# Local stage: the first pair of exponentials between ScalarE's two head-out copies; q and k written and read on SP ahead of both groups of P

## The reference

```
for l in range(DEPTH):                       # DEPTH = 2
    h = shift_token(x)
    q, k, v = split(h @ wqkv)                # 8 heads of 64
    q, k = rotary_xpos(l2norm(q) * qs, l2norm(k) * ksc)
    o = softmax(mask(8 * q @ k.T)) @ v       # windows of 128, each sees itself and the one before
    x = x + o @ wo
    h = layernorm(shift_token(x)) * lg + lb
    a, g = split(h @ w1 + b1)
    x = x + (a * gelu(g)) @ w2 + b2
```

## Time and profile before

| | |
|---|---|
| median of 3 runs | 4911.67 us (4908.47 to 4913.42) |
| the profiled execution | 4915.73 us, span 4913.9 us |
| PE busy | 4346.3 us, 88% of the span |
| DVE, ACT, POOL busy | 67%, 59%, 47% |
| DMA | 728.62 MB, mean 148 GB/s |

### The profile page before, as it was taken

The page is one execution under the profiler, slowest core; times in us unless marked ns, Lnnn a source line. Parts: engine busy times, 40 slices in busy tenths (PEclk is TensorE's granted clock), DMA queues, the critical chain, the costliest instruction groups (busy, mean ns, idle before and its releaser), DMA issues. The chain is left out here.

```text
span 4913.9 us, 281580 instructions
## 1 busy us (share of the span) xinstructions
PE 4346.3 (88%) x114072; PEld 3665.2 (75%) x114072; DVE 3295.8 (67%) x10277; ACT 2920.9 (59%) x8550; POOL 2290.3 (47%) x3196
## 2 busy tenths in 40 slices
PE   7888888678888888665999999999999999999998
PEld 6888888668888888653777777777777777777776
DVE  4666666578888888474666666666666666666664
ACT  5777777534444444253666666666666666666665
POOL 1222222257777777302444445444445555555553
PEclk8999999879999999787999999999999999999999
DMA  3334343467777777595666666666676667676665
GB/s 88 88 94 97 90 94 95 103 147 163 164 167 163 164 166 163 143 296 160 153 156 156 154 154 152 151 152 155 162 176 159 160 163 164 161 162 161 158 158 121
DMA packets 1454099, 728.62 MB, mean 148 GB/s; under 512 B 676624, under 2 KB 1398288, under 8 KB 1452816
## 3 DMA queue, kind: packets, MB, share of 16 engines
q1 hardware_dynamic: 1402448, 652.89, 57.6%
q10 hardware_dynamic: 51392, 73.02, 5.1%
HBM read 410.48 MB, written 315.15 MB: 148 GB/s over the span
## 5 line engine op out<-in xcount | busy, mean ns | idle before, releaser
L2354 ACT ACTIVATE l_prob<-l_prob,l_nb,l_rq 128x160 f32<-128x160 f32 x1024 | 518.4, 509 | 14.3 <-DVE l_nb L2189 14.3
L2015 POOL TENSOR_TENSOR l_k<-l_kn,l_tab 128x512 f32<-128x512 f32 x128 | 162.1, 1267 | 613.2 <-DVE l_kn L2163 613.2
L2031 POOL TENSOR_TENSOR l_prob<-l_prob,l_rinv 128x320 f32<-128x320 f32 x512 | 362.8, 719 | 76.3 <-DVE l_rinv L2171 76.1
L2559 PE MATMUL lD<-l_hid,w 128*128 128x128 f32 x3072 | 363.9, 275 | 0.0
L2559 PEld LDWEIGHTS lD<-l_hid,w 128*128 128x128 f32 x3072 | 353.3, 192 | 0.0
L2551 PEld LDWEIGHTS lA<-l_hn,w 128*128 128x128 f32 x2048 | 243.1, 195 | 110.3 <-POOL l_hn L2049 61.1
L2198 DVE STREAM_TRANSPOSE l_pb<-l_prob 128x320 f32<-128x320 f32 x512 | 250.6, 498 | 104.1 <-POOL l_prob L2031 104.1
L2025 POOL TENSOR_TENSOR l_qr<-l_q 128x512 f32<-128x512 f32 x128 | 162.4, 1269 | 329.0 <-DVE l_q L2127 329.0
L1097 POOL TENSOR_TENSOR sc_aqx<-sc_late,sc_headmask 128x256 f32<-128x256 f32 x256 | 172.1, 672 | 278.3 <-PE sc_Y L1190 275.0
L1173 PE MATMUL sc_AB<-sc_aq,sc_bkx 32*32 32x32 f32 x16384 | 258.6, 198 | 39.9 <-POOL sc_bkx L1097 29.7
L497 POOL TENSOR_TENSOR rk<-rk,bkraw 128x256 f32<-128x256 f32 x64 | 54.6, 872 | 477.8 <-DVE bkraw L383 477.8
(11 more groups left out here) (273 smaller groups left out, 13217.1 us busy)
## 6 DMA issues: line engine op xcount, KB each, us to landing
l_pT<-scratch_pz SPq DMA_DIRECT2D x1024, 128.0 KB, 3.7
scratch_pz<-l_pb SPq DMA_DIRECT2D x256, 320.0 KB, 3.0
scratch_qkz<-l_qk SPq DMA_DIRECT2D x128, 512.0 KB, 3.2
l_qkT<-scratch_qkz SPq DMA_DIRECT2D x512, 128.0 KB, 3.8
scratch_cm<-cm SPq DMA_DIRECT2D x64, 512.0 KB, 4.1
sc_early<-scratch_cm ACTq DMA_DIRECT2D x59, 512.0 KB
scratch_tok<-vt SPq DMA_DIRECT2D x512, 48.0 KB, 1.8
scratch_part<-sc_att SPq DMA_DIRECT2D x64, 384.0 KB
```

Of the source, the lines that this page charges most:

```text
L2015: tt(k1[s][:], kn[s][:], wide(2, slice(0, DH)), ALU.mult)
L2031: tt(prob[s][:, pair], prob[s][:, pair], rinv[s][:, pair].unsqueeze(2).broadcast_to([P, 2, SPAN]), ALU.mult).then_inc(Q["pn"][s].sem, 1)
L2354: last_ = nc.scalar.activation(prob[s][:, h], prob[s][:, h], ACT.Exp, scale=rq8[s][:, h:h + 1], bias=nb[s][:, h:h + 1], accum_out=sums[s][ ...
L2559: last_ = mm(bank[s][3][:, c * P:(c + 1) * P], w2[:, m, c * P:(c + 1) * P], hid[s][:, m], start=(c == 0 and m == 0), stop=(c == CC - 1 and ...
```

## The change

On SP the q and k write comes before both writes of P, and the q and k read before both reads of P. On ScalarE `exponent` 0 stands between `head_out` 0 and `head_out` 1.

```diff
@@ sync: half @@
-                    write_p(s, u, 0)
                     if within(un):
                         write_qk(o, un)
+                    write_p(s, u, 0)
                     write_p(s, u, 1)
-                    read_p(s, u, 0)
                     if within(un):
                         read_qk(o, un, wn)
+                    read_p(s, u, 0)
                     read_p(s, u, 1)
@@ scalar: half @@
                         head_out(o, um, 0)
+                    exponent(s, u, 0)
+                    if mlp:
                         head_out(o, um, 1)
-                    exponent(s, u, 0)
                     exponent(s, u, 1)
```

## The result

The changed kernel takes 4853.51 us, the median of 4 runs (4852.8 to 4857.42), beside 4910.07 for the kernel before in the same session (4905.67 to 4913.42). The ratio is 0.9886, with a 95% interval of 0.987 to 0.9902: faster, by 57 us. The forecast was 4856.

A forecast was written before the change was run, and what follows sets the result against it. PE, busy 88%, is bound by how early each local-stage half's projection can start, with P1 late. Period 20.18 to 19.68 over 127 halves saves 63.5 us, giving 4848; plus 8 for late landings, 4856; range 4840 to 4895.

The forecast's parts named there:

- rival 1: Local stage: PE's wait for P becomes a wait of 0.3 to 0.6 us for ACT's copy; 4840 to 4880, chance 0.70.
- `l_nb` sits under POOL's lock: VectorE's `l_nb` ends with POOL's rotation of k, 2.68 us into the half, which sets the floor of exponent 0.
- The part behind the projection: From the projection's start to the half's end, alike in both layers: 15.42 and 15.58 us, taken as unchanged.
- the term for late landings: Noise in when DMA reads land, P0 having 0.8 us to spare: half of today's 17.4 us, 8 us added.
- The sum of 19.68 x 127: New period of a half, 4.18 + (15.42 + 15.58) / 2 = 19.68 us against 20.18, over 127 halves: 63.5 us.
- Signs that the prediction named: `l_pT` wait under 15 us, ACT copy wait about 0.5 a half, projection at 4.2, period 19.7; wrong if values 0 await P0.
- When P lands: SP's DMA queue at 218 GB/s: P1 lands 1.5 us earlier, P0 with 0.8 us to spare before values 0.
- the bytes hold it, not the issues: P1's landing is set by 2.42 MB queued from the q/k write, 11.1 us at 218 GB/s, not by SP's issuing.
- Rival 2: Reads only partly in time: P0 some tenths late every half, mean 0.25 us, half the gain left; 4880 to 4901, chance 0.13.
- The swap alone gains nothing: ACT part, exponent 0 moved between the two `head_out` copies: no gain alone, free only while P1 is late.
- it holds back part of what SP gives: Without the ACT part the copy could start as soon as values 3 end, at 2.8 to 3.2 us.
- Rival 3: Slower: q/k write's early issue frees nothing, values 0 wait 0.7 us for P0 every half; 4937, chance 0.05.

The follow-up runs named there:

- e1_sp_only: Kernel before with only SP's new order of writes and reads, ScalarE's order as before: 4847.41 us, ratio 0.9867.
- e5_nb_one_input: Changed kernel with `l_nb` made by two one-column tensor_scalar instructions instead of one two-column tensor_tensor: 4855.22 us, ratio 0.9881.
- e7_rotate_order: Changed kernel with POOL's three products of rotate_k reordered, the two short ones first and the long one last: 4879.4 us, ratio 0.993.
- e15_xa_last: e3_early_write_only with the load of the residual x issued on SP behind both writes of P: 4866.75 us, ratio 0.9906.
- e3_early_write_only: Changed kernel with SP's reads back in the old order (P0, q/k, P1), q/k write still ahead of P0: 4880.16 us, ratio 0.9933.
- e4_early_read_only: Changed kernel with SP's writes back in the old order (P0, q/k, P1), reads still q/k, P0, P1: 5020.39 us, ratio 1.022.
- e8_k_turned_first: Changed kernel without the swap; `turn_k` ahead of `attended`, q/k write ahead of SP's window load, q/k read between P's writes: 4833.15 us, ratio 0.9835.
- e2_act_only: Kernel before with only ScalarE's new order (the swap), SP's order as before: 4914.28 us, ratio 1.0003.
- e10_both: e8_k_turned_first (no swap) with the `l_nb` of e5_nb_one_input: 4807.81 us, ratio 0.979.

## Why the prediction was right, and where its sizes were off

**The wait that takes over (rival 1)** is shown. P1 comes in time, exponent 0 starts when `l_nb` ends, and the copy behind it releases PE. I had 2.72 for exponent 0, 3.74 to 4.11 for the copy and 4.18 for the projection. The half above shows 2.72, 3.74 to 4.09 and 4.15, and the mean over all halves is 4.15 (4.69 before). e1_sp_only shows that it is the swap that sets 4.15 in layer 0, and e5_nb_one_input and e7_rotate_order that `l_nb` sets it in turn: with `l_nb` at 2.59, 2.66 and 2.81 the projection is at 4.09, 4.15 and 4.30 (means of all halves). In layer 1 the copy ends last by 0.04 us only. The prediction had PE's own work end at 3.54 + 0.37 = 3.91 there and the maxima of pair 1 in time; they are not, and without the swap the projection stands at 4.10. So what rival 1 says holds in full for one layer of the two.

**That `l_nb` sits under POOL's lock** was argued from two rows. The ends of all 381 long `l_nb` show it, and e5_nb_one_input supports it: with one column of one tile plus a column as scalar, `l_nb` finishes while POOL still runs. The prediction cited the Trainium skill, SBUF — State Buffer, section Who interferes with whom; by its rule that a VectorE instruction with at most one SBUF input, outside the 2-port modes, does not contend (if a column taken as a scalar is no such input) the two new instructions should keep their length under POOL's work, and they do: 0.34 us for both under `l_k`, against 0.44 for the one instruction of the change. How much earlier `l_nb` could be was not part of the forecast. With this remedy it is 0.09 us.

**The part behind the projection** was taken as 15.42 and 15.58, and it is in the middle: medians of the two kinds of halves are the same numbers. Its means are 15.58 and 15.71, because values 0 now and then wait for P0. That is about 0.14 us a half, 18 us in all, where the term for late landings had 8. The sum of 19.68 x 127 plus 8 us corresponds to a period of 19.74. Measured is 19.78.

**That the total came out within 3 us is in part luck.** A fall of the period from 20.18 to 19.78 over 127 halves is 51 us, and the local stage gave 56. The rest comes from halves at its ends, which the prediction did not look at: the first takes 22.28 us instead of 24.98. They make up for what the late P0 cost beyond its term of 8 us. What lies ahead of the local stage took 2 us less in this execution.

**Signs that the prediction named.** Exponent 0, the projection and the period are as it said. It allowed PE under 15 us of waits for `l_pT` in 2300 us; there are 16.5 and 13.5. It named a wait of values 0 for P0 as a sign that it is wrong, and there are 22 of them, up to 2.1 us. It had about 0.5 us a half for the wait on ACT's copy; PE's matmuls wait 10.5 us in all, 0.09 a half, and its weight load 46.1, 0.4 a half.

**When P lands** is the step that was mis-sized. I let bytes queue at 218 GB/s, so that 0.52 MB fewer in front of the reads were worth 2.4 us, and P1's landing moved 1.5 us towards the projection. It moved 0.6: P1 lands about 17.7 behind the projection's start (median; 18.3 before), and P0 at 15.1 to 15.2 instead of 14.6, which leaves it 0.3 of slack and not 0.8. What the runs show in its place is that P1 follows the first read at a distance that changes little with the bytes. Reads start at 7.8 before, 7.5 in the change, 8.07 in e15_xa_last (layer 1), 8.73 in e3_early_write_only (layer 1) and 9.27 in e4_early_read_only; P1 lands 10.5, 10.2, 9.9, 9.6 and 9.7 later. In e8_k_turned_first and the three kernels built on it the reads start at 5.8 to 6.0 and P1 lands 10.9 later. Getting the q/k write out of the way saved 0.3 us of that distance and 0.3 us of the start.

Two readings of the prediction failed with this. The rate was no constant: over the reads of the changed kernel the DMA engines are nearly as full as before (share 0.97 against 1.03) and move 191 GB/s, not the 218 of the earlier trace rows:

```profile
3235.00:3245.00 10.00, 9.71 (x125) 9.03 (x125) 6.63 (x23) 6.10 (x15) 3.20 (x4) 1.00 0.97 191
```

And "the bytes hold it, not the issues" is too strong. SP issues the last read of P1 5.4 to 5.5 us behind the first read in the change (5.9 before, 7.1 to 7.4 in e8_k_turned_first), and P1 lands 4.5 to 4.7 us behind that (4.5 before, 3.5 to 3.7 in e8_k_turned_first). In the change 1.91 MB move between first read and landing in layer 0 and 2.18 in layer 1, and the distance is the same in both (medians). No run changes the pace of the issues alone, so how much of the distance is theirs stays open.

By an estimate from the fit in the Trainium skill, DMA: Bandwidth & Descriptors, section Anatomy of one DMA — SWDGE (gpsimd) path, which is for another path of issue, the 0.52 MB would be worth 1.2 us, nearer to the measured 0.6 but still twice it.

The error cost little because two waits stand behind one another. P1 had 0.7 us before it would outlast ACT's copy and used up most of it. Rival 2, which took P0 late by tenths in every half, is true at about half its size in the mean (22 halves of some 116 wait), which is where the 18 us come from.

**"The swap alone gains nothing"** was right (e2_act_only), and so was "it holds back part of what SP gives". Its price depends on P: 6 to 14 us in the change, over 20 once P is in time. The prediction named no number for it, and my expectation of 35 us for e1_sp_only was too high because I had left out that the row maxima come next in layer 1, and that P1 is late by more than its median in some halves.

**Rival 3** needed the q/k write to free nothing. Leaving that write at its old place does produce it (e4_early_read_only, slower by 2.2%), so the two edits on SP lean on one another: the reads may go first only because the write does.

Open: how SP's issues and the bytes share the distance from the first read to P1, and why the rate falls to 191 GB/s with the engines full, when the q/k write no longer lies beside the reads; and the 0.3 us of P1 in layer 1 of e15_xa_last. Other ways to free `l_nb`, such as a copy of `l_nrq` in PSUM, were not tried.

## What to carry to other kernels

When a wait is removed, list what ends next, with its slack, for each engine that feeds the same instruction: here P1, ACT's copy and the row maxima lay within some tenths of a microsecond, and their order differed between the two layers, so partial remedies gave 57, 67 or 78 us and all of them without the swap 105. Work put in an engine's idle time is free only as long as that idle time is; the swap cost nothing beside the old SP order and over 20 us beside the best one. In a queue of transfers through HBM, look at when the first read may begin and what small load or write stands in front of the write that it needs, before counting bytes.

## What the runs showed of the hardware

The VectorE instruction `l_nb`, of two columns with both inputs in SBUF, takes 0.16 us where no POOL operation is under way and up to 1.26 where one is, with a median of 0.432 in the changed kernel. Whenever it takes over 0.20 it ends 0.01 to 0.02 us behind a POOL instruction. Its mean over 2500 to 4800 us grew from 0.336 us before to 0.470, though nothing about it was edited. In e10_both the instruction of one column is never held. The first row is the changed kernel's `l_nb`, the second that of e10_both, duration in ns as minimum, median and maximum:

```profile
L2189 DVE TENSOR_TENSOR l_nb<-l_mx,l_nrq x465: 160/432/1259, 2500.1 to 4795.2; 128x2 f32<-128x2 f32 x155
```

```profile
L2190 DVE TENSOR_SCALAR l_nb<-l_mx,l_nrq x936: 201/210/217, 2513.8 to 4765.7; 128x1 f32<-128x1 f32 x188
```

A 128 KB load just ahead of a 320 KB write in SP's queue delayed that write's landing by about 0.6 us (8.56 and 8.47 against 7.89), although its issue takes only about 0.35 (medians of 0.34 to 0.38). The reads, 128 KB each, landed at a median of 3.8 us after their issue for P in the change (3.7 before), and for q and k at 3.2, where they now come first, against 3.8 between those of P before.
